# Item norm of the second 128 features on ScalarE in eight operations per group, in place of two on VectorE

## What is computed

```
# layer 0: adapter by item, residual, layer norm
hidden = gelu(x @ down_W.T + down_b)
hidden = hidden @ expert_W[id].T + expert_b[id] + domain_emb[id]
x = layer_norm(hidden @ up_W.T + up_b + x) * ln_gamma + ln_beta

# layer 1: norms, style, two of eight experts per token
h = (x - mean(x, -1)) * rsqrt(var(x, -1) + 1e-5) * ln_g + ln_b
h_norm = (h - mean(h, tokens of the item)) * rsqrt(var(h, tokens of the item) + 1e-8)
h = h_norm * gamma[item] + beta[item]
gates, idx = top_2(softmax(h @ router_w))
out = x + sum over the two of gate * (relu(h @ w1[e] + b1[e]) @ w2[e] + b2[e])
```

## Time and profile before

| | before |
|---|---|
| median of 3 runs | 640.93 us (640.7 to 641.24) |
| the profiled execution, its own time | 642.02 us |
| its span in the profile | 640.2 us |
| busy: TensorE, VectorE, ScalarE, GpSimd | 542.2, 402.6, 278.0, 247.6 us |
| dense stage up to the first tile of the experts | about 239 us |

### The profile page before, as it was taken

One profiled execution on the slowest core, in us unless ns is written; L12 is line 12 of the kernel. 1 busy time (PEld: TensorE's weight loads), 2 busy tenths in 40 slices (PEclk: granted clock), 3 DMA queues, 4 the chain that ended last, 5 costly groups with the idle time before them and its releaser, 6 DMA issues.

```text
span 640.2 us, 15839 instructions
## 1 busy us (share of the span) xinstructions
PE 542.2 (85%) x4370; PEld 461.7 (72%) x4371; DVE 402.6 (63%) x1431; ACT 278.0 (43%) x628; POOL 247.6 (39%) x208
## 2 busy tenths in 40 slices
PE   5986878888814308999999999999999999999992
PEld 4864665667614306888888888888888888888772
DVE  2566988998896534565656565656565655655571
ACT  2557656666643204343525343434434343434350
POOL 2010388778788520222323333323333323233221
PEclk8689778776865557999999999999999999999997
DMA  9363435565341244433333333333333424232321
GB/s 262 138 193 121 164 129 194 177 196 185 118 153 67 88 154 118 51 42 58 41 58 41 58 47 52 55 44 58 41 58 41 60 39 65 38 44 37 50 33 19
DMA packets 78082, 57.41 MB, mean 90 GB/s; under 512 B 51346, under 2 KB 71699, under 8 KB 77907
## 3 DMA queue, kind: packets, MB, share of 16 engines
q1 hardware_dynamic: 62610, 37.31, 21.4%
q0 software_dynamic: 13296, 17.83, 16.5%
q10 hardware_dynamic: 2146, 1.91, 1.2%
HBM read 23.18 MB, written 24.55 MB: 75 GB/s over the span
## 4 chain that ended last, share of the span: by engine, by line
PE 60%; DMA 1%; issue 1%; POOL 0%; ACT 0%; SPq 0%; DVE 0%; POOLq 0%; DVEq 0%
PE banks L1240 31%; PE banks L1256 29%; DMA out<-yg,token 1%; DMA rT<-queues 1%; POOL out L1205 0%; ACT yg L1304 0%; SPq L1177 0%; DVE yb L1373 0%; POOLq L1214 0%; DVEq L1373 0%; SPq L1179 0%; POOLq L84 0%
## 5 line engine op out<-in xcount | busy, mean ns | idle before, releaser
L1205 POOL DMA_INDIRECT out<-yg,token x71 | 117.0, 1648 | 287.3 <-ACT yg L1304 177.2
L1240 PE MATMUL banks<-rT,w_high 128*128 128x256 f16 (+1 forms) x1248 | 198.0, 266 | 23.9 <-DMA rT<-queues 23.4
L1240 PE MATMUL banks<-rT,w_low 128*128 128x256 f16 (+1 forms) x624 | 163.9, 265 | 0.0
L1256 PE MATMUL banks<-w_high,hid_high 128*128 x568 | 154.9, 273 | 0.8
L1256 PE MATMUL banks<-w_high,hid_low 128*128 x568 | 154.8, 273 | 0.0
L1256 PE MATMUL banks<-w_low,hid_high 128*128 x568 | 154.8, 273 | 0.0
L1288 ACT ACTIVATE hid<-banks,feat 128x256 f32<-128x256 f32 (+1 forms) x312 | 119.4, 455 | 65.6 <-PE banks L1240 52.9
L1240 PEld LDWEIGHTS banks<-rT,w_high 128*128 x1248 | 115.0, 98 | 43.0 <-issue 25.4
L1304 ACT ACTIVATE yg<-yb,gate 128x256 f32<-128x256 f32 x71 | 32.6, 501 | 186.0 <-DVE yb L1373 186.0
L1342 DVE TENSOR_TENSOR hid_low<-hid,hid_high 128x512 f16<-128x512 f32 (+1 forms) x156 | 101.1, 648 | 5.4
L1340 DVE CAST hid_high<-hid 128x512 f16<-128x512 f32 (+1 forms) x156 | 67.8, 434 | 45.4 <-issue 22.8
(11 more groups left out here) (179 smaller groups left out, 613.0 us busy)
## 6 DMA issues: line engine op xcount, KB each, us to landing
stage<-expert_w SPq DMA_DIRECT2D x32, 512.0 KB
xb<-x SPq DMA_DIRECT2D x8, 512.0 KB
out<-rb SPq DMA_DIRECT2D x8, 512.0 KB, 3.2
queues<-pad_row SPq DMA_DIRECT2D x5, 260.0 KB
out<-yg,token POOLq DMA_INDIRECT x71, 3.8
queues<-pad_row ACTq DMA_DIRECT2D x4, 260.0 KB
queues<-h_rows,slot POOLq DMA_INDIRECT x64
b<-exp_b SPq DMA_DIRECT2D x1, 1024.0 KB, 5.1
```

What stands on the lines that cost most here:

```text
L1205: nc.gpsimd.indirect_dma_start(out=out, out_offset=bass.IndirectOffsetOnAxis(ap=token[:, i.par, s:s + 1], axis=0), in_=yg[:, i.par, s, :], ...
L1240: last = nc.tensor.matmul(ps_in(i, c), w[:, at], features(i)[:, v, k, :], start=(n == 0), stop=(n == 3 * DC - 1))
L1256: last = nc.tensor.matmul(ps_out(i.par)[:, s, :], v[:, i.par, c, s * P:(s + 1) * P], w[:, at], start=(n == 0), stop=(n == 3 * FC - 1))
```

## The change

Item norm's second half goes to ScalarE as well: `item_norm` loops over both halves, each with its eight operations of 64 columns, and adds one to `h_ready` per half. The two operations on VectorE and their two semaphores go. The order of all else stays.

```diff
                 def route_and_back(i):
-                    pe.wait_ge(h_ready, i.g + 1)
-                    pe.wait_ge(h_rest_ready, i.g + 1)
+                    pe.wait_ge(h_ready, (i.g + 1) * DC)
...
                 def item_norm(i):
-                    sc.wait_ge(aff_ready[0], (i.g + 1) * 3)
-                    for b in range(GI):
-                        v = hT[:, 0, b * T:(b + 1) * T]
-                        last = nc.scalar.activation(v, v, ACT.Identity, scale=aff_a[:, 0, b:b + 1],
-                                                    bias=aff_c[:, 0, b:b + 1])
-                    last.then_inc(h_ready, 1)
+                    for c in range(DC):
+                        sc.wait_ge(aff_ready[c], (i.g + 1) * 3)
+                        for b in range(GI):
+                            v = hT[:, c, b * T:(b + 1) * T]
+                            last = nc.scalar.activation(v, v, ACT.Identity, scale=aff_a[:, c, b:b + 1],
+                                                        bias=aff_c[:, c, b:b + 1])
+                        last.then_inc(h_ready, 1)
...
                     if k == 0:
                         dve.wait_ge(rsT_ready, i.g * DC + (c + 1))
-                        wait(dve, h_ready, i.g)
+                        wait(dve, h_ready, i.g * DC)
...
-                def item_norm_rest(i, add):
-
-                    v = hT[:, 1, :].rearrange("p (b t) -> p b t", t=T)
-                    if not add:
-                        dve.wait_ge(aff_ready[1], i.g * 3 + 1)
-                        V.tensor_tensor(v, v, bcast(aff_a[:, 1, :], 2, [P, GI, T]), ALU.mult).then_inc(scaled_ready, 1)
-                    else:
-                        dve.wait_ge(scaled_ready, i.g + 1)
-                        dve.wait_ge(aff_ready[1], (i.g + 1) * 3)
-                        V.tensor_tensor(v, v, bcast(aff_c[:, 1, :], 2, [P, GI, T]), ALU.add).then_inc(h_rest_ready, 1)
...
                     step(s3, item_scale, 1, 1)
-                    step(s3, item_norm_rest, False)
                     step(s3, item_scale, 1, 2)
-                    step(s3, item_norm_rest, True)
                     step(s2, norm_shift)
```

More of the change, by code:

```diff
@@ L309, in dense @@
              "n_ready", "nT_done", "hT_ready"))
-        (stT_ready, item_step, var4_ready, rsT_ready, scaled_ready, h_ready, h_rest_ready, logits_done,
+        (stT_ready, item_step, var4_ready, rsT_ready, h_ready, logits_done,
          logits_copied, back_done, high_ready, low_ready) = (sem(n) for n in (
-             "stT_ready", "item_step", "var4_ready", "rsT_ready", "scaled_ready",
-             "h_ready", "h_rest_ready", "logits_done", "logits_copied", "back_done", "high_ready", "low_ready"))
+             "stT_ready", "item_step", "var4_ready", "rsT_ready",
+             "h_ready", "logits_done", "logits_copied", "back_done", "high_ready", "low_ready"))
         aff_ready = [sem("aff_ready0"), sem("aff_ready1")]
```

## The result

| | before | after |
|---|---|---|
| median of the runs | 640.82 us (638.36 to 641.24, 4 runs) | 663.75 us (662.52 to 664.64, 4 runs) |
| ratio to before | | 1.0365 (95%: 1.0333 to 1.0397) |
| the profiled execution, its span | 642.02, 640.2 us | 664.64, 662.8 us |
| VectorE, ScalarE, GpSimd busy | 402.6, 278.0, 247.6 us | 392.8, 299.0, 241.0 us |

The change makes the kernel 3.65% slower, 23 us; 663 us was forecast. VectorE, the busiest engine of the dense stage, has 9.8 us less to do, and the kernel pays 23 us for it. An fp32 matmul call shows as two matmuls in the rows: the logits are eight calls and x16.

A forecast was written before the change was run, and what follows sets the result against it. VectorE's work and GpSimd round trips were taken to bound groups, with the item norm to TensorE chain taking over; group costs 2.2 + 14.8 + 2.66 + 2.55 = 22.2 us on the median 640.93 gave 663 us, range 655 to 667.

The forecast's parts named there:

- What binds: Dense stage: VectorE's own work and two GpSimd round trips set a group's period; the chain through TensorE has 0.64 us slack.
- The removal: VectorE before line 848: 1.37 us fewer operations per group buy nothing; line 848 comes 1.0 us earlier, taken as nothing.
- the second rival: VectorE at line 848: the freed GpSimd port decides, 3.9 us faster, median 637 us; chance 0.03.
- The addition: ScalarE's item norm: eight more operations per group, sixteen ending after 5.42 us; logits start 2.66 us later.
- TensorE's clock: Logits and transposes on TensorE: the longer idle gap brings half clock, 5.42 us in place of the fourth group's 4.32.
- The rival with 4.32 us: Logits and transposes on TensorE keep their earlier clock: 16.5 us slower, median 657.4 us; chance 0.16.
- The sum: Item norm's start to line 943, all eight groups: 2.2 + 14.8 + 2.66 + 2.55 = 22.2 us slower.
- The slower rival: TensorE's ranks, next transposes and adapter take over as the chain at low clock: 26 us slower, 667 us; chance 0.07.
- VectorE's new wait at `low`: Sign in the profile after: VectorE waits about 0.7 us for line 681 in every group.
- the faster rival: Same as the second rival: VectorE's earlier line 848 counts, 3.9 us faster, median 637 us; chance 0.03.

The follow-up runs named there:

- the addition alone: Kernel after with VectorE's two operations put back at their place, working on two spare tiles nobody reads: 665.22 us, ratio to before 1.0354.
- the removal alone: Kernel after without the second half's scale and shift, so VectorE's two operations are gone and ScalarE keeps eight: 636.89 us, ratio to before 0.9918.
- Half a dose: Kernel before with four of the second half's eight items on ScalarE, the other four on VectorE over 256 columns: 651.97 us, ratio 1.0127.
- the wide operation: Kernel after with the second half's eight ScalarE operations of 64 columns replaced by one of 512: 644.94 us, ratio to before 1.0076.
- Filling the gap: Kernel after with four extra thrown-away matmuls of 512 columns on TensorE ahead of its item norm wait: 653.74 us, ratio to before 1.0181.
- the run with eight operations on VectorE: Kernel before with VectorE's two wide operations replaced by eight of 64 columns that scale and shift at once: 644.84 us, ratio 1.0038.
- the second one: Profile of the unchanged kernel after, run once more beside the run with twelve ScalarE operations: 663.96 us, ratio to before 1.0339.

## Why the prediction was right

- **What binds.** Before, VectorE's order sets the middle groups' period, and a second chain, item norm, TensorE, line 681, `low`, runs beside it with little slack. Lengthening that chain cost its full length less the slack in every group. The slack of 0.64 us is the fourth group's; with the 0.04 us of each hand-over it is 0.60 there, and 0.13, 0.47, 0.73 and 0.77 in groups 2, 3, 5 and 6. The forecast did not need it group by group, since `low` came 8.69 to 8.79 us after item norm's start in all five.
- **The removal** was taken at nothing beside the addition, and the addition alone measured the same as both. GpSimd's 1.0 us came as read from the earlier trace rows, and line 848 came 0.98 us earlier. That the removal alone landed near the second rival's 3.9 us is in part luck: the sum has 0.6 us in each of groups 2 to 6, and its trace has 1.0 us gained or 0.5 to 0.6 lost, by TensorE's clock.
- **The addition**: 5.42 us worked out, 5.41 in the profile. Half a dose and the wide operation put the cost on the series' length.
- **TensorE's clock**: 5.42 us for logits and transposes was taken from the seventh group. Of groups 1 to 6 after, four show it, the third has 4.84 and the first 3.83. Filling the gap brought the clock back and 10 us. The rival with 4.32 us fell. That the longer idle time by itself lowers the clock is not shown: in the run with eight operations on VectorE the second group's weight loads took 3.49 us behind 2.20 us of idle time, and in the run with the removal alone the sixth group's took 1.86 us behind 2.93.
- **The sum**: 22.2 us forecast, 22.2 in the table. So close a match is luck, since two errors cancel: groups 2 to 6 together gave 15.4 in place of 14.8 (the 0.2 us taken off in each for full clock showed in the third alone), and group 1 gave 1.68 in place of 2.2. Group 7 gave 2.66 as said and group 8 2.54 for 2.55.
- **The slower rival** with TensorE's later work as the chain fell too: from the third group's `low` to the fourth's item norm it is 128.74 - 117.20 = 11.54 us before and 136.17 - 124.62 = 11.55 after, and VectorE waits for the ranks in no group.
- **Where it was off**: VectorE's new wait at `low` is 0.70 or 0.71 us, as said, in groups 2, 6 and 7, and 0.88 or 0.89 in the others. Its busy time fell by 9.8 us, not 11: the multiplication of the earlier trace rows runs from 129.76 to 130.44, while the operation ahead of it ends at 129.84 and the one behind it starts at 130.36, so 0.16 us of it were no busy time of their own. What I had not drawn out is that the clock limits the faster rival as well, as the run with the removal alone shows.
- **Open**: which of groups 1 to 6 get full clock differs between executions (group 3 has a part of it in the profile after, group 4 in the second one). No run fixes what decides that, and the length of TensorE's idle time alone does not.

## What to carry to other kernels

Before moving work off the busiest engine, look at what waits for the result: here the moved work went from a place where it ran beside another engine to the end of that engine's series, and every group paid for it. An operation with one scale and shift per partition has to be issued for every item, and its fixed part is paid each time: on ScalarE eight of 64 columns take 2.76 us and one of 512 takes 0.80; on VectorE eight take 1.88 us, and two wide ones with a broadcast operand 1.58. And where TensorE idles ahead of a chain that others wait for, its clock is part of the price: the kernel before with that gap filled in its last two groups, by a count that ends about when the wait does, measured 0.46% faster, of which the trace gives most to the filling. A count that is too long delays the work behind it and gives the gain away.

## What the runs showed of the hardware

- One ScalarE operation of 512 columns takes 799 ns, one of 64 columns 425 ns, and in a series one starts every 333 ns.
- Eight fused scale-and-shift operations of 64 fp32 columns take VectorE 1.88 us, 0.23 each; the two wide operations over the same data take 1.58 us from the first one's start to the second one's end, with a small one between them.
- Two small GpSimd operations take 0.69 and 1.59 us beside VectorE operations with two tensor inputs, whether these work on `hT` or on spare tiles, and 0.26 and 1.04 without. Beside eight operations with one tensor input they take 0.25 and 1.10. Who starts first matters: where GpSimd's second one began 0.01 us ahead of VectorE's addition (171.63 and 171.64 above; groups 2 and 6 of the run with the addition alone are alike) it took 1.04 us and the addition 0.73 in place of 0.69.
- Sixteen weight loads of the logits take 1.86 us when extra matmuls had filled TensorE's wait (granted clock 1.00), and 3.49 us behind an idle time of 4 us (0.50). Shorter idle times are seen with either: 2.20 us ahead of 3.49, 2.93 us ahead of 1.86.
